# One accumulating DMA per step in place of two VectorE additions, with three places for queries and three for kept values

## What is computed

```python
x = x + 0.5 * _L0_ffn_ref(_layernorm(x), ...)        # 8 experts, the best 2 of each row, and a shared one
x = x + _L0_attn_ref(_layernorm(x), ...)
x = x + 0.5 * _L0_ffn_ref(_layernorm(x), ...)

# in _L0_attn_ref, for K*H = 256 channels and M = 8 angles each:
phi = k_val[..., None] * theta
re_k, im_k = (jnp.cos(phi), jnp.sin(phi))
cs = jnp.cumsum(concatenate([p_w, pw5 * re_k, pw5 * im_k]), axis=1)      # over time
out_re = jnp.sum(state_re * q_re + state_im * q_im, axis=-1)              # sum over the M angles
out_im = jnp.sum(state_im * q_re - state_re * q_im, axis=-1)
```

## Time and profile before

| | |
|---|---|
| median of 3 runs | 1280.1 us (1279.31 to 1285.77) |
| the profiled execution | 1298.13 us, its span 1296.8 us |
| busy in it | PE 1005.9, DVE 719.3, ACT 594.9, POOL 447.9 us |
| DMA | 155.13 MB, mean 120 GB/s |

### The profile page before, as it was taken

One profiled execution on the slowest core, in us unless ns is written; L12 is line 12 of the kernel. 1 busy time (PEld: TensorE's weight loads), 2 busy tenths in 40 slices (PEclk: granted clock), 3 DMA queues, 4 the chain that ended last, 5 costly groups with the idle time before them and its releaser, 6 DMA issues.

```text
span 1296.8 us, 10501 instructions
## 1 busy us (share of the span) xinstructions
PE 1005.9 (78%) x3168; PEld 538.4 (42%) x3168; DVE 719.3 (55%) x1162; ACT 594.9 (46%) x1015; POOL 447.9 (35%) x432
## 2 busy tenths in 40 slices
PE   6999889964986768887983569976986796969774
PEld 3446555422443434453431234454453442436542
DVE  3401000087888695987898989997996830200000
ACT  4334333333535575567532345376758720413332
POOL 4263443203634343232110134344452312244442
PEclk9999989986988897888896869988998998889997
DMA  8974554424156465486143742665676435035454
GB/s 283 377 188 87 101 86 69 78 84 124 30 108 177 95 124 107 105 234 157 49 111 85 175 139 47 153 151 129 124 189 146 78 49 106 33 74 96 92 90 55
DMA packets 60587, 155.13 MB, mean 120 GB/s; under 512 B 10962, under 2 KB 10962, under 8 KB 58358
## 3 DMA queue, kind: packets, MB, share of 16 engines
q0 software_dynamic: 29568, 60.90, 27.7%
q1 hardware_dynamic: 30966, 93.58, 23.8%
HBM read 99.74 MB, written 58.88 MB: 122 GB/s over the span
## 4 chain that ended last, share of the span: by engine, by line
DMA 32%; PE 32%; DVE 12%; ACT 8%; issue 7%; POOL 7%; SPq 1%; POOLq 0%; ACTq 0%; DVEq 0%
DMA x_rows<-ys,into_i 12%; DMA out_rows<-ys,into_i 11%; PE hps L757 6%; PE yps L769 6%; PE misc L888 4%; DMA xs<-x_normal,rows_i 4%; PE yps L826 3%; PE hps L810 3%; POOL slots L1557 3%; DVE run L1374 2%; PE misc L854 2%; DMA xin<-in_x 2%; ACT ys L1004 2%; PE misc L845 1%; ACT xin L1025 1%
## 5 line engine op out<-in xcount | busy, mean ns | idle before, releaser
L826 PE MATMUL yps<-w_all,hidden_sb 128*128 x368 | 202.5, 679 | 57.2 <-ACT hidden_sb L991 56.8
L810 PE MATMUL hps<-w_all,hidden_sb 128*128 x736 | 186.6, 400 | 1.2 <-ACT hidden_sb L974 1.1
L1374 DVE TENSOR_TENSOR_SCAN run<-pwx,trig 128x512 f32<-128x512 f32 x128 | 149.4, 1208 | 61.8 <-ACT trig L1075 61.3
L810 PEld LDWEIGHTS hps<-w_all,hidden_sb 128*128 128x128 f32 x736 | 145.4, 204 | 44.9 <-issue 27.4
L1569 POOL DMA_INDIRECT xs<-x_normal,rows_i x92 | 111.3, 1210 | 91.9 <-PE xps L801 65.2
L1004 ACT ACTIVATE ys<-yps,slots 128x512 f32<-128x512 f32 x92 | 62.9, 685 | 169.3 <-PE yps L826 72.3
L1582 POOL DMA_INDIRECT x_rows<-ys,into_i x46 | 79.4, 1727 | 169.6 <-ACT ys L1004 81.7
L1582 POOL DMA_INDIRECT out_rows<-ys,into_i x46 | 82.7, 1798 | 155.4 <-DMA out_rows<-ys,into_i 79.6
L826 PEld LDWEIGHTS yps<-w_all,hidden_sb 128*128 128x128 f32 x368 | 73.9, 213 | 128.7 <-issue 126.5
L757 PE MATMUL hps<-xnT,sw_sb 128*128 128x512 f32 x256 | 121.3, 623 | 3.2 <-ACT hidden_sb L964 1.7
L801 PE MATMUL xps<-ident,xs 128*128 128x128 f32 x368 | 60.7, 297 | 77.4 <-DMA xs<-x_normal,rows_i 75.9
(11 more groups left out here) (199 smaller groups left out, 1531.3 us busy)
## 6 DMA issues: line engine op xcount, KB each, us to landing
qx<-q_cols SPq DMA_DIRECT2D x128, 256.0 KB
x_normal<-xin SPq DMA_DIRECT2D x32, 256.0 KB, 3.8
w_all<-in_w_experts SPq DMA_DIRECT2D x8, 1024.0 KB, 9.8
xin<-x_rows SPq DMA_DIRECT2D x32, 256.0 KB, 6.5
turns_sb<-in_w_out SPq DMA_DIRECT2D x3, 1536.0 KB, 7.5
xin<-in_x SPq DMA_DIRECT2D x16, 256.0 KB, 4.2
x_rows<-ys POOLq DMA_DIRECT2D x16, 256.0 KB, 4.5
q_cols<-xin SPq DMA_DIRECT2D x16, 256.0 KB
```

The costliest lines, as they stand in the source:

```text
L810: t = PE.matmul(hps[:, bank, 0:H], xT[:, j % 2, c, :], w_all[:, bass.ds(expert[j] + c * H, H)], start=c == 0, stop=c == KC - 1)
L826: t = PE.matmul(yps[:, bank, :], hb[:, j % 2, ec, :], w_all[:, bass.ds(expert[j] + (KC * H + ec * D), D)], start=ec == 0, stop=ec == EC - 1)
L1374: t = VE.tensor_tensor_scan(run[:, c, :], pwx[:, n // M, :], trig[:, n % 2, c, :], 0.0, ALU.mult, ALU.add)
```

## The change

`sum_parts` is left out in all steps but the very last, `FINAL`. Both parts of a step now land in the step's place of `qx` (imaginary part first, since the real part overwrites what it reads), and POOL issues one DMA of 128x1024 from there to `outT`, with addition (`add_step`, stage `c_acc`). That DMA waits for the step's two additions and for the accumulating DMA before it. A place of `qx` is free when that DMA has landed, so there are three places (NQX = 3). To make room in SBUF, `kval` has three places in place of four (NK = 3), and `cmp_a`, `cmp_b` and `chunks_sb` share one tile `cmp_sb`. The planner is given the new stage and costs, and writes new orders for all engines.

```diff
+        cmp_sb = sb("cmp_sb", [P, T])
+        cmp_a = cmp_sb[:, 0:T // 2].rearrange("p (t e f) -> p t e f", e=E, f=E)
+        cmp_b = cmp_sb[:, T // 2:T].rearrange("p (t e f) -> p t e f", e=E, f=E)
+        chunks_sb = cmp_sb
...
-        NK = 2 * HALVES
+        NK = 3
...
-        NQX = 2
+        NQX = 3
...
+            last = STEPS_OF[i - NQX]
+            used = [("POOL", ("c_acc", *last), 4.8) if last[1] % M else ("DVE", ("c_sum", *last))] if i >= NQX else []
...
-            piece("DVE", ("c_sum", b, n), 2.8 if m else 1.4, ("DVE", ("c_times", b, n)),
+            piece("DVE", ("c_sum", b, n), 1.4 if (b, n) != FINAL else 2.8, ("DVE", ("c_times", b, n)),
...
+            if m and (b, n) != FINAL:
+                piece("POOL", ("c_acc", b, n), 1.0, ("DVE", ("c_sum", b, n)),
+                      *([("POOL", ("c_acc", b, n - 1), 4.8)] if m > 1 else []))
...
             def add_parts(b, n):
-                re2, im2 = trig[:, n % 2, :, :], qx[:, n % NQX, :, :]
-                re = outT[:, half, 0, :] if m == 0 else re2[:, 0, :]
-                im = outT[:, half, 1, :] if m == 0 else im2[:, 0, :]
+                re2, im2 = trig[:, n % 2, :, :], queries(b, n)
+                re, im = [outT[:, half, i, :] if m == 0 else im2[:, i, :] for i in range(2)]
...
-                vec.wait_ge(*real_made.at((b, n)))
-                VE.tensor_tensor(re, re2[:, 0, :], re2[:, 1, :], ALU.add).then_inc(*added.of((b, n, 0)))
                 vec.wait_ge(*imag_made.at((b, n)))
                 VE.tensor_tensor(im, im2[:, 0, :], im2[:, 1, :], ALU.subtract).then_inc(*added.of((b, n, 1)))
+                vec.wait_ge(*added.at((b, n, 1)))
+                VE.tensor_tensor(re, re2[:, 0, :], re2[:, 1, :], ALU.add).then_inc(*added.of((b, n, 0)))
...
+            def add_step(b, n):
+                half, m = divmod(n, M)
+                pool.wait_ge(*added.at((b, n, 0)))
+                i = out_summed.order.index((b, n))
+                if i > 0:
+                    pool.wait_ge(*out_summed.at(out_summed.order[i - 1]))
+                GE.dma_start(outT[:, half, :, :], queries(b, n),
+                             accum_op=ALU.add).then_inc(*out_summed.of((b, n)))
...
             def load_query(b, n):
-                if n >= NQX:
-                    sp.wait_ge(*(out_summed if (n - NQX) % M else added).at((b, n - NQX, 1)))
+                if i >= NQX:
+                    last = STEPS_OF[i - NQX]
+                    sp.wait_ge(*(out_summed.at(last) if last[1] % M else added.at((*last, 0))))
```

More of the change, by code:

```diff
@@ L315, in plan_job @@
             piece("PE", ("chunks", q), 1.6, *kept_rows, *start[:1], bank=[("xps", ("ACT", ("chunks", q)))])
-            piece("ACT", ("chunks", q), 0.6, ("PE", ("chunks", q)), *([("PE", ("logits", q - 1))] if q else []))
+            piece("ACT", ("chunks", q), 0.6, ("PE", ("chunks", q)), *([("PE", ("logits", q - 1))] if q else []),
+                  *([("DVE", ("place", g - 1))] if g and not second else []))
             piece("PE", ("logits", q), 1.3, ("ACT", ("chunks", q)), *start[2:], bank=[("xps", ("DVE", ("rank", q)))])
@@ L398, in plan_head @@
                 s = ("a_mem", b, i)
-                free = [("DVE", ("c_turn", b - 2, i * M + M - 1))] if i < HALVES and b >= 2 else []
+                free = [("DVE", ("c_turn", *divmod((HALVES * b + i - NK) * M + M - 1, STEPS)))] \
+                    if i < HALVES and HALVES * b + i >= NK else []
                 free += [("DVE", ("a_den", b - 1))] if i == HALVES and b else []
@@ L423, in plan_step @@
             free = [("DVE", ("c_sum", *STEPS_OF[i - 2]))] if i >= 2 else []
-            piece("SP", ("c_query", b, n), 0.9, *[("SP", ("a_q", b, half * QH + g), 2.5) for g in range(QH)], *free)
+            last = STEPS_OF[i - NQX]
+            used = [("POOL", ("c_acc", *last), 4.8) if last[1] % M else ("DVE", ("c_sum", *last))] if i >= NQX else []
+            piece("SP", ("c_query", b, n), 0.9, *[("SP", ("a_q", b, half * QH + g), 2.5) for g in range(QH)], *used)
             piece("DVE", ("c_turn", b, n), 1.3, ("DVE", ("a_mem", b, half)), *free, *([] if i else [("DVE", ("w_soft", 1))]))
@@ L444, in plan_tail @@
                       bank=[("misc", ("DVE", s))])
-                piece("DVE", s, 1.5, ("PE", s), ("DVE", ("c_sum", b, half * M + M - 1)))
+                last = b, half * M + M - 1
+                piece("DVE", s, 1.5, ("PE", s), ("POOL", ("c_acc", *last), 4.8) if last != FINAL else ("DVE", ("c_sum", *last)))
                 piece("SP", s, 1.8, ("DVE", s))
@@ L611, in macaron @@
         imag_made = signal("s_imag", BN)
-        added = signal("s_added", [(b, n, i) for b, n in BN for i in range(2)])
-        out_summed = signal("s_out_summed", [(b, n, i) for b, n in BN if n % M for i in range(2)])
+        added = signal("s_added", [(b, n, i) for b, n in BN for i in (1, 0)])
+        final_summed = signal("s_final_summed", [0])
         out_scaled = signal("s_out_scaled", BHALF)
@@ L632, in macaron @@
         y_added = signal("s_y_added", BLOCKS, 16)
+        out_summed = signal("s_out_summed", [s for s in BN if s[1] % M and s != FINAL], 16)
         small_loaded = signal("s_small_loaded", range(3), 16)
```

58 lines of the change are left out of this document (31 added, 27 removed).

## The result

The changed kernel takes 1324.7 us (median of 4 runs, 1322.1 to 1327.7); the kernel before took 1282.9 beside it (1279.3 to 1291.8). The ratio is 1.032, 95% interval 1.025 to 1.038. It is slower, and above the range of 1246 to 1303. The profiled execution has a span of 1324.8 us.

A forecast was written before the change was run, and what follows sets the result against it. DVE was taken to bound the kernel between the groups, with DVE and PE waiting for each other beside them. DVE -49, ring +9 and tail +27 gave -13 us, so 1267 us; the range was 1246 to 1303.

The forecast's parts named there:

- DVE's saving: Work taken off DVE: 66.6 us of additions removed less new waits, net 49 us; a step of about 7.2 us.
- the 0.11 us for a dependent wait: On DVE, an addition waiting for the instruction in front costs 0.11 us; two in each of 64 steps, 14.1 us.
- the sum: The forecast's total for the span: DVE -49, ring +9, tail +27, so -13 us and 1267 us.
- The slices of the page: Reading of the profile before: DVE at 8 or 9 tenths from the eleventh to the thirty-second slice.
- The tail: From the last step to `hidden` of job 7: 94 us in place of 67, costing 27 us.
- The output rows: Batch 3's rows on PE, counted as 15.5 us of the work behind the last step.
- The gap before job 7's turning: PE had nothing from 1085.3 to 1105.8 in the kernel before; job 6 would now cover that wait.
- the first rival: Beside the groups DVE's gain becomes idle time waiting for ACT: 1276 to 1286 us, chance 0.17.
- The DMA's contention: Each step's DMA takes 3.2 us of the shared 16 engines; its effect on other transfers counted as nothing.
- adds landing in 8 us or more: Sign of being wrong in the DMA: blocks' adds land this late in group 2, which grows past 199 us.
- The ring and POOL's queue: Reuse of the three `qx` places, slowed by waits in POOL's queue: 18 to 60 us lost, 9 us taken.
- POOL's queue holds the steps back: Rival: step DMAs stand behind waiting adds, queries come late, 45 us lost, 1303 us; chance 0.27.

The follow-up runs named there:

- e10: e1 with the four additions of the kernel before in place of two dependent ones and one of 128x1024; 0.987 of the kernel before.
- e1: Changed kernel with its orders and places, but each step's running sum made by one 128x1024 addition on DVE, no accumulating DMA; 0.984 of the kernel before.
- e2: Changed kernel with the 55 running sums ahead of the final step and their waits left out; 0.966 of the kernel before.
- e12: e9 with 1 MB in each of the 55 transfers that nobody waits for; 1.004 of the kernel before.
- e9: e2 plus 55 plain transfers of 512 KB of weights to unused DRAM, issued after the step's additions, landings not waited for; 0.977 of the kernel before.
- e4: Changed kernel whose DMA sums read unchanging weights, so a qx place is free after the step's additions; other waits kept; 1.012 of the kernel before.
- e3: Changed kernel whose DMAs each add only 64 of the 512 KB, all waits kept; 0.985 of the kernel before, 1276.7 us.
- e7: Changed kernel's order with DMA sums only in 14 steps between groups 1 and 2, the other 41 sums on DVE; 1.004 of the kernel before.
- e5: Changed kernel's places and merged sum on DVE, with the DMA sums also out of the plan, so another order; 1.011 of the kernel before.
- e6: Changed kernel whose DMA adds only the real half, 256 KB in place of 512, imaginary sums left out; 1.003 of the kernel before.

## Why the prediction was wrong

*DVE's saving* was right. 49 us were reckoned; the pages say 719.3 and 665.0, so 54. The step in a run was to be 7.2 us and is 7.14, and the 0.11 us for a dependent wait, which the sum took from one row, is there again (0.11 and 0.13, e10). The Trainium skill (VectorE: DVE Perf Modes, section "The DRAIN you can't avoid") says that a semaphore after each instruction costs nothing extra, measured on copies. For an instruction that waits for the one right in front of it these rows disagree, with 0.11 and 0.13 us. The slices of the page were read roughly, without harm to the sum: 5 of the 22 slices said to be at 8 or 9 tenths are at 5 to 7.

*The tail* came out right as far as it went: 94 us from the last step to `hidden` of job 7, measured 93. That is in part luck. The output rows were taken as 15.5 us, from a piece of the chain with 36 products; there are 48, and PE's timeline of the kernel before has them all:

```profile
1069.71 20.76 PE L888 MATMUL misc<-turns_sb,tail_sb 128*128 128x512 f32 x48
1103.18 1.97 PE L722 MATMUL xps<-ident,xin 128*128 128x128 f32 x8 [12.71 <-ACT xin L1025]
```

So the work was counted 5 us short, and the 4 us of idle that the sum added nearly made up for it, though PE had hardly any (91.5 of 93 us busy). The gap before job 7's turning was 12.7 us of idle, not the 20.5 from 1085.3 to 1105.8. And the tail was counted from one side. The blocks and rows that PE does there had left the middle, and that was put at nothing. e1 has the new order as a whole, and its last step ends 44 us earlier, with more work on DVE. The order as a whole gives 1.6%, where the sum had it at +27 us. This error spoke for a slower kernel, and the result was slower still.

*What DVE's saving is worth* was too high, as the first rival had it. Taking up to 73 us from DVE brought 27 (e1 to e2). From 371 to the last step, DVE's scans then wait 28.1 us for ACT's sines where they waited 4.9, the tail's products 11.1 where it was 4.6, and the statistics 6.2 for `xin` where it was 3.4. The sum took each us of 49 as one.

*The DMA's contention is the step that failed:* "I count nothing for it in the sum and keep it for the upper end." The amount was right: 3.2 us of the 16 engines for a step were taken, 2.4 to 4.0 as bounds, 2.5 measured; the share beside group 2 was to be 0.83 and is 0.78. Its price was not: it was put at nothing. Almost this load, with nobody waiting for its landing, costs 49 us (e2 to e12), of which 34 (e9 to e12) are load alone and the rest may in part be POOL's wait for the additions. I had looked at the chain of the blocks' adds in group 2, where 136 of 199 us leave room, and named adds landing in 8 us or more as the sign of being wrong; they land in 7.2. But the load lengthens the landings of rows and queries too, beside group 1 and between the groups as well: `xin` lands in 10.7 us where it took 6.9, and such landings are links of the long chain.

*The ring and POOL's queue* were under-sized: 9 us were taken, 18 to 60 named as lost. The ring alone is 25 us (changed kernel less e4). With small DMAs, ring, queue and waits together are 27 us (e2 to e3). The rival "POOL's queue holds the steps back" was nearest, with 45 us lost: its mechanism is seen in the 100 us in which POOL stood at its own predecessor's landing, in the 29 us in which the products waited for queries, and in e7's DMA that was issued 19 us after its products began. Ring and waits for a landing are 35 us in the list below, the load 34 to 49, so both are real and which is larger isn't shown; against the sum, the load was missed by more (34 or more against nothing, 25 against 9). The rival also looked in one direction only: POOL's waits for the sums also hold the blocks.

Put together, by ratios times 1283 us: order and places -21, DVE's sums left out -23 (27 by the times of that one chip), load with POOL's wait for the additions +49, the waits of POOL and the scaling for a landing +10, ring +25; that is +40, and the medians differ by 42. The steps from e2 on were taken in this order, and the order matters: with waits first (e3) these are 25 and the bytes 60. Each has an uncertainty of 6 to 12 us, so the +10 can hardly be told from nothing; and between e12 and e4 the transfer changes too, from plain to accumulating and from 2.25 to 2.7 us of the 16 engines.

What stays open: why the order that the planner makes around the DMA sums is better than the others (e1 against e5); what POOL's wait for the additions costs by itself; and through which of the lengthened landings the load works most; e12 wrote to DRAM while the DMA sums stay in SBUF, so its 49 us are those of a load of the same length, not of the same transfer.

Of the versions that make the whole sums, e1 and e10, with the sums on DVE and the changed kernel's order, are the ones that beat both kernels: 0.984 and 0.987 of before, and so about 0.954 of the changed kernel (0.984 / 1.032).

## What to carry to other kernels

An engine's work handed to the DMA engines is paid in the landings of everything else: before counting it as nothing, ask which loads stand on the long chain, what share the engines have already, and take a run with the same load and no waits. Give that run a partner that keeps the place in the queue and has no load, or the two can't be told apart. A transfer in a queue that is worked through in order holds what stands behind it, and it is itself held by what stands ahead; with a ring of few places both come back to the engine that was to be relieved. And when a change moves work from one stage to another, count what it leaves as well as what it adds: separate the order from the operation by a kernel that has the new order and the old operation.

## What the runs showed of the hardware that I hadn't expected

- An accumulating DMA from SBUF to SBUF takes 2.5 us of the 16 engines for 512 KB, 1.4 for 256 KB and 0.65 for 64 KB, each to about 0.15 us (the changed kernel, e6, e3; 2.7 for 512 KB in e4). A plain one from SBUF to DRAM takes 1.3 for 512 KB (e9) and 2.25 for 1 MB (e12).
- The cost of load on the DMA engines grew faster than the load: 1.3 us a transfer cost 1.1% (e9 over e2), 2.25 us 3.8% (e12 over e2), and the fixed cost of issuing them and of POOL's waits is in both.
- POOL's addition of 128x1024 takes 2.9 us (DVE's 1.2), and slows DVE's instructions in the mean: the scans from 1.21 to 1.57 us, L1382 from 0.75 to 1.25. The Trainium skill (SBUF — State Buffer, section "SBUF: two separate sides") says that a DVE instruction with two SBUF inputs and a GpSimd instruction that reads SBUF exclude each other on a shared pair of ports; the scans, with two inputs, agree, with 0.36 us on the mean and a longest of 3.76. L1380, with one tensor input and a scalar from SBUF, went from 0.48 to 0.66 as well, which that sentence doesn't cover.
